# Four graph networks in one kernel: one of DVE's two inputs moved from SBUF to PSUM in layer 0 and the attentions

## The reference, cut to what matters

```
L0: msg = relu(x[src] + edge_attr @ We + be);  h = x + segment_sum(msg, dst);  gelu(h@W1+b1)@W2+b2
L1: four attentions (8 heads; 16, 32, 16, 64 channels) with batch norms between:
      e = leaky_relu(s_src[src] + s_dst[dst]);  m = segment_max(e, dst);  ex = exp(e - m[dst])
      alpha = ex / segment_sum(ex, dst)[dst];   out = segment_sum(h[src] * alpha, dst)
L2: five steps of m = (h @ W[type])[src];  a = segment_sum(m, dst);  h = gru(a, h)
L3: relu(segment_sum((h @ W16[type])[src] * weight, dst))
```

## Time and profile before

| stage | from, to (us) | us | POOL busy | PE busy | DVE busy | granted PE clock |
|---|---|---|---|---|---|---|
| layer 0 | 75 to 1170 | 1095 | 848 | 684 | 640 | 0.57 |
| attention a, pass | 1325 to 2423 | 1098 | 851 | 497 | 388 | 0.73 |
| attention b, pass | 2677 to 3823 | 1146 | 900 | 638 | 481 | 0.79 |
| attention c, pass | 4099 to 5184 | 1085 | 838 | 497 | 371 | 0.73 |
| attention d, pass | 5439 to 7282 | 1843 | 1463 | 1125 | 709 | 0.77 |
| layer 2 (steps) | 7640 to 9350 | 1710 | 0 | 1650 | 355 | 0.95 |
| layer 3, pass | 9445 to 10452 | 1007 | 761 | 314 | 333 | 0.62 |

### The profile page before, as it was taken

One profiled execution on the slowest core, in us unless ns is written; L12 is line 12 of the kernel. 1 busy time (PEld: TensorE's weight loads), 2 busy tenths in 40 slices (PEclk: granted clock), 3 DMA queues, 4 the chain that ended last, 5 costly groups with the idle time before them and its releaser, 6 DMA issues. The chain is left out here.

```text
span 10484.5 us, 120372 instructions
## 1 busy us (share of the span) xinstructions
PE 6178.0 (59%) x43869; PEld 5573.6 (53%) x43869; DVE 4046.9 (39%) x8325; ACT 2190.6 (21%) x5754; POOL 6356.2 (61%) x5804
## 2 busy tenths in 40 slices
PE   4666534444455545444446666665699999993333
PEld 3555434443455534444436665665488888862322
DVE  6656433335344453333453334333422211223333
ACT  0000022221233320322213333333011100111111
POOL 5777677776777775777767777776400000007776
PEclk7555567775787875777757777777599999975666
DMA  5555522220333321222124444443087788751111
GB/s 176 173 188 173 80 53 59 58 59 17 94 102 101 102 61 30 58 59 58 47 62 121 121 120 120 120 120 97 4 321 289 280 315 308 288 195 28 27 27 27
DMA packets 451604, 1241.90 MB, mean 118 GB/s; under 512 B 157362, under 2 KB 233139, under 8 KB 411041
## 3 DMA queue, kind: packets, MB, share of 16 engines
q1 hardware_dynamic: 213988, 744.49, 20.2%
q0 software_dynamic: 237024, 489.72, 17.9%
HBM read 1096.42 MB, written 137.35 MB: 118 GB/s over the span
## 5 line engine op out<-in xcount | busy, mean ns | idle before, releaser
L1122 PE MATMUL ps<-pool 128*106 128x128 f32 (+2 forms) x19344 | 2707.5, 311 | 266.5 <-DVE pool L1029 266.5
L1122 PEld LDWEIGHTS ps<-pool 128*106 128x106 f32 (+2 forms) x19344 | 2678.1, 193 | 279.0 <-DVE pool L1029 278.6
L441 POOL DMA_INDIRECT pool<-t,ACC x416 | 392.6, 944 | 1963.0 <-issue 1963.0
L1080 ACT ACTIVATE ACC<-ps 72x256 f32 (+1 forms) x2418 | 1010.3, 418 | 2271.2 <-PE ps L1122 2058.5
L718 POOL DMA_INDIRECT cnt_d<-pool x806 | 1064.8, 1321 | 540.2 <-PE ps L1299 221.5
L1102 PE MATMUL ps<-ident,pool 128*128 128x128 f32 (+1 forms) x204 | 96.3, 472 | 2080.7 <-DVE pool L989 2080.7
L1102 PEld LDWEIGHTS ps<-ident,pool 128*128 128x128 f32 (+1 forms) x204 | 37.0, 181 | 2129.6 <-DVE pool L989 2129.6
L1147 POOL DMA_INDIRECT pool<-d_h,srcT_s x806 | 943.1, 1170 | 245.5 <-issue 231.2
L1147 POOL DMA_INDIRECT pool<-b_h,srcT_s x806 | 899.4, 1116 | 245.5 <-issue 234.9
L1147 POOL DMA_INDIRECT pool<-a_h,srcT_s x806 | 850.9, 1056 | 245.6 <-issue 245.0
L1147 POOL DMA_INDIRECT pool<-c_h,srcT_s x806 | 836.8, 1038 | 245.6 <-issue 245.3
(11 more groups left out here) (258 smaller groups left out, 7910.5 us busy)
## 6 DMA issues: line engine op xcount, KB each, us to landing
ACC<-cnt_d SPq DMA_DIRECT2D x206, 1600.0 KB, 8.5
pool<-cnt_d SPq DMA_DIRECT2D x104, 1600.0 KB, 8.6
cnt_d<-pool SPq DMA_DIRECT2D x31, 3200.0 KB, 14.6
pool<-key_d SPq DMA_DIRECT2D x62, 832.0 KB, 6.3
pool<-seg_d SPq DMA_DIRECT2D x204, 64.5 KB
cnt_d<-pool POOLq DMA_INDIRECT x806, 2.5
pool<-a_h,srcT_s POOLq DMA_INDIRECT x806
pool<-b_h,srcT_s POOLq DMA_INDIRECT x806
```

What stands on the lines that cost most here:

```text
L441: g.indirect_dma_start(out=gb[b][:, k, :], out_offset=None, in_=table, in_offset=bass.IndirectOffsetOnAxis(ap=idx[:, c:c + 1], axis=0)).th ...
L1080: a.activation(win[:, 0:NPL, bass.ds(reg, 128)], pl[0].rearrange("p (i c) -> p i c", c=128), ACT.Copy).then_inc(*(tile_out if last else A) ...
L1122: mm = t.matmul(o, gbr[:, tile % RT, M * i:M * i + M], oh, start=True, stop=True)
```

## The change

In layer 0 the one-hots read `count0`, a copy of `iota` in bank 5 of PSUM, and the multiplicities read `unit0`, ones in that bank. Bank 5 is then no longer free for products: `tensor_products` and `vector_add_windows` take a number of banks, five in layer 0 and six in layer 3 as before. In the attentions the one-hots read a copy of `iota` in bank 7, and the weights times the multiplicities go to `wp` in bank 7; the multiplies of the rows (L1029) read them there, and one more copy brings them to the rows. PE's turned scores (`eR`, `dR`) and turned weights and maxima (`pC`, `mC`) now share bank 6, and the turn of `sdl` waits for `packed` as well. Each attention and layer 0 copy `iota` once at their start.

```diff
+        count0, unit0 = ps[5][:, 0:128], ps[5][:, 128:256]
         def vector_multiplicity(gi):
-                                       scalar=keyT[:, c:c + 1], in1=onec[:, 0:1].to_broadcast([128, 128]),
-                                       op0=ALU.is_equal, op1=ALU.mult, accum_out=cmul[:, c:c + 1]).then_inc(*V.one())
+                                       scalar=keyT[:, c:c + 1], in1=unit0, op0=ALU.is_equal, op1=ALU.mult, accum_out=cmul[:, c:c + 1]).then_inc(*V.one())
-        def vector_add_windows(gi, FA, o, added):
+        def vector_add_windows(gi, FA, o, added, banks):
-                bk = (NC_ * gi + c) % 6
+                bk = (NC_ * gi + c) % banks
         def tensor_products(gi, msg, oh, FA, o, added, banks):
-                if u >= 6:
-                    t.wait_ge(added.sem, u - 5)
+                if u >= banks:
+                    t.wait_ge(added.sem, u - banks + 1)
-                    mm = t.matmul(ps[u % 6][0:FA, ...
+                    mm = t.matmul(ps[u % banks][0:FA, ...
         def vector_l0():
+            v.tensor_copy(count0, iota[:, :]).then_inc(*V.one())
+            v.memset(unit0, 1.0).then_inc(*V.one())
+            v.wait_ge(*V.now())
-                vector_onehot(gi, oh0, o_l0, iota[:, :])
+                vector_onehot(gi, oh0, o_l0, count0)
             def vector_table():
+                v.tensor_copy(count, iota[:, :]).then_inc(*V.one())
+            eR, dR = ps[6][:, 0:128], ps[6][:, 128:256]
+            pC, mC = ps[6][:, 256:384], ps[6][:, 384:512]
+            count, wp = ps[7][:, 0:128], ps[7][:, 128:256]
             def vector_edge_onehot(c, n):
-                v.tensor_tensor(out=ohr[:, k:k + n, :], in0=iota[:, :].unsqueeze(1).to_broadcast([128, n, 128]),
+                v.tensor_tensor(out=ohr[:, k:k + n, :], in0=count.unsqueeze(1).to_broadcast([128, n, 128]),
             def vector_edge_weights(gi):
-                v.tensor_tensor(out=rows[:, :, 0:8], in0=ps[6][:, 0:8 * n].rearrange("p (k h) -> p k h", h=8),
+                wk = wp[:, 0:8 * n].rearrange("p (k h) -> p k h", h=8)
+                v.tensor_tensor(out=wk, in0=pC[:, 0:8 * n].rearrange("p (k h) -> p k h", h=8),
                 v.wait_ge(*V.now())
+                v.tensor_copy(rows[:, :, 0:8], wk).then_inc(*V.one())
-                                        in1=rows[:, q:q + n_, 0:8].unsqueeze(3).to_broadcast([128, n_, 8, C]),
+                                        in1=wk[:, q:q + n_, :].unsqueeze(3).to_broadcast([128, n_, 8, C]),
             def tensor_turn_scores(gi):
                 t.wait_ge(lists_g[b].sem, l0[b] + 32 * (gi // 2 + 1))
-                t.transpose(ps[7][0:8 * n, 128:256], sdl[:, b, 0:8 * n], ident[:, :])
                 t.wait_ge(packed.sem, pk0 + gi + 1)
-                t.transpose(ps[7][0:8 * n, 0:128], sc[:, b, 0:8 * n], ident[:, :]).then_inc(*eT.one())
+                t.transpose(dR[0:8 * n, :], sdl[:, b, 0:8 * n], ident[:, :])
+                t.transpose(eR[0:8 * n, :], sc[:, b, 0:8 * n], ident[:, :]).then_inc(*eT.one())
```

More of the change, by code:

```diff
@@ L451, in vector_onehot, with tensor_products @@
                             op=ALU.is_equal).then_inc(*o["oh"].one())
-        def tensor_products(gi, msg, oh, FA, o, added):
+        def tensor_products(gi, msg, oh, FA, o, added, banks):
             b = gi % 2
@@ L456, in tensor_products @@
                 u = NC_ * gi + c
-                if u >= 6:
-                    t.wait_ge(added.sem, u - 5)
+                if u >= banks:
+                    t.wait_ge(added.sem, u - banks + 1)
                 for i in range(m):
-                    mm = t.matmul(ps[u % 6][0:FA, 128 * i:128 * i + 128], msg[:, k0 + i, :], oh[b][:, k0 + i, :],
+                    mm = t.matmul(ps[u % banks][0:FA, 128 * i:128 * i + 128], msg[:, k0 + i, :], oh[b][:, k0 + i, :],
                                   start=True, stop=True)
@@ L998, in vector_edge_logits @@
                 v.wait_ge(eT.sem, et0 + gi + 1)
-                v.tensor_tensor_scan(out=e, data0=sg[:, 0:128], data1=ps[7][0:r, 128:256], initial=iniT[0:r, gi:gi + 1],
+                v.tensor_tensor_scan(out=e, data0=sg[:, 0:128], data1=dR[0:r, :], initial=iniT[0:r, gi:gi + 1],
                                      op0=ALU.add, op1=ALU.max).then_inc(*V.one())
                 v.wait_ge(*V.now())
-                v.tensor_tensor(out=e, in0=e, in1=ps[7][0:r, 0:128], op=ALU.add).then_inc(*V.one())
+                v.tensor_tensor(out=e, in0=e, in1=eR[0:r, :], op=ALU.add).then_inc(*V.one())
                 v.wait_ge(*V.now())
@@ L1108, in tensor_turn_back @@
                 t.wait_ge(logit.sem, lg0 + gi + 1)
-                t.transpose(ps[6][:, 128:128 + r], ml[0:r, :], ident[0:r, 0:r])
+                t.transpose(mC[:, 0:r], ml[0:r, :], ident[0:r, 0:r])
                 t.wait_ge(prob.sem, pb0 + gi + 1)
-                t.transpose(ps[6][:, 0:r], et[0:r, b, :], ident[0:r, 0:r]).then_inc(*mxT.one())
+                t.transpose(pC[:, 0:r], et[0:r, b, :], ident[0:r, 0:r]).then_inc(*mxT.one())
             def tensor_tile(tile):
@@ L1567, in vector_step_pass @@
                 if gi:
-                    vector_add_windows(gi - 1, D, o, added)
-            vector_add_windows(NG - 1, D, o, added)
+                    vector_add_windows(gi - 1, D, o, added, 6)
+            vector_add_windows(NG - 1, D, o, added, 6)
             v.wait_ge(*added.now())
@@ L1586, in tensor_step_pass @@
                 t.wait_ge(o["msg"].sem, gi + 1)
-                tensor_products(gi, gb[gi % GB], oh, D, o, added)
+                tensor_products(gi, gb[gi % GB], oh, D, o, added, 6)
             t.wait_ge(*added.now())
```

8 lines of the change are left out of this document (4 added, 4 removed).

## The result

The changed kernel takes 9876.11 us (median of four runs, 9873.66 to 9878.19) against 10490.87 us for the kernel before beside it. The ratio is 0.9413, with a 95% interval of 0.9397 to 0.943. The profiled execution has a span of 9874.2 us against 10484.5: 610.3 us less.

What follows compares the result with a forecast made beforehand. POOL sets the pace, its gathers held by DVE instructions reading SBUF twice. Attentions 495 + layer 0 10 - 2 = 503 us off 10485.76 gives 9983, and 9985 as the runs' median; range 9890 to 10070 us.

Steps and rivals of the forecast that it cites:

- What bounds the kernel: Layer 0 and the four attention passes: POOL's gathers and scatters, busy plus 0.30 us each, set the pace of all five.
- That one input in PSUM ends the holds: Attention one-hots and L1029 stop holding POOL's gathers: 63, 125, 64 and 243 us in a to d, 495 in all.
- rivals 4 and 5: 4: L1029 still holds POOL, 10280 us, chance 0.05; 5: POOL held by DVE's writes or its long run, 10540, 0.02.
- What PSUM costs DVE: Layer 0's multiplicities with a PSUM input: no extra time taken; bounds 10% of 351 ns each, 23 us in the stage.
- rival 2: Layer 0: a PSUM input costs each multiplicity 70 ns, 0.9 us a group, 46 us less gain: 10031 us; chance 0.06.
- The slack of the chain: Attention passes: the chain from scores to tiles grows 0.5 us a group but stays hidden, 3.7 us left in d.
- rival 3: Attention d becomes bound by its chain, 50 to 100 us less gain: 10035 to 10085 us; chance 0.07.
- I take 10: Layer 0's gain of 10 us: with five banks PE's loop of 17.8 us, not POOL's 16.2, sets the pace.
- rival 1: POOL sets layer 0's pace too, as PE's clock rises or the loop closes earlier: gain 577, 9911 us; chance 0.12.
- lower bound of the scans: Attention passes: holds left by scans and similar short instructions at 0 us a group, +48 us on the gain.
- 12 us a pass: Attentions: holds left by L1004, L1006, L1009 and L1012, still reading SBUF twice, 0.24 us a group x 51.
- what lies between the stages: A loss of 2 us in all: the chain's added 0.5 us shows behind the last group of each pass.

Runs made afterwards that it cites:

- experiment 5: Changed kernel with the attentions' one-hots, or else only the multiplies' weights, read from SBUF again; 11473.29 and 11338.94 us beside the changed kernel's 11272.19, in the long condition.
- experiment 2: Kernel before with five banks in place of six for layer 0's products, nothing else changed; 10488.62 us beside 10482.69.
- Experiment 4: Changed kernel with two idle 128 x 128 copies on DVE ahead of the first scan of every group in the attentions; 9875.03 us.
- long condition: Chips or times at which every kernel took 7 to 8% longer; kernel before 11230 to 11370 us in place of 10490; the change's ratio there 0.9918.

## Why the prediction was wrong in size and right in kind

**What bounds the kernel: right.** POOL's busy time fell, its idle time moved by under 1 us in each of the five stages, and the end followed.

**That one input in PSUM ends the holds: right,** rivals 4 and 5 fall. The gathers that took 1.68 to 2.42 us are 0.94 to 0.97, and experiment 5 brings either hold back alone. In layer 0 the one-hots and the multiplicities were changed together; the gathers that began during a multiplicity took 1.03 us in the mean before (176 of them) and 0.945 after (163). The rule of the Trainium skill that two SBUF inputs contend with a GpSimd instruction that reads SBUF ("SBUF — State Buffer", "Who interferes with whom") agrees; its inferred sentence that `tensor_tensor` doesn't stall DMAs does not (279 us of holds by L1029's form).

**What PSUM costs DVE: right at nothing,** rival 2 falls. L313 takes 342 ns with `unit0` in PSUM, where L311 took 351; L1042 1212 against 1220; L450 1878. The 65 ns more that the prediction estimated from the Trainium skill ("VectorE: DVE Perf Modes", section on the TRN2 errata) are in none of these lines.

**The slack of the chain: right,** rival 3 falls. DVE still waits for the gather ahead of the scores in each of 50 groups a pass, though less (us, times), to be set beside 380.8 in the earlier trace rows:

```profile
  DMA pool<-d_h,srcT_s: 527.6, 50
...
  DMA pool<-b_h,srcT_s: 221.7, 50
```

In b 7.6 us a group became 4.4, for a period shorter by 134 / 50 = 2.7 and the half microsecond of the chain.

**First step that failed: layer 0, "I take 10".** The structure was right: one bank less makes the last chunk wait for the third chunk's adds, L609 or L614 releases 51 groups, and at the lower level the turn takes 17.8 us. Mis-sized was the duration of L609 in it. I took 5.81 us from a turn in which PE had idled 1.70 us ahead of its last two chunks, and named as a bound, with a chance of 0.12, that it might run at 2.4 GHz without that gap. It did so for the most part in 33 of the first 51 groups: 3.1 to 3.8 us, 3.60 in the turn shown (not the 2.9 of the prediction's half, and so a loop of mostly 15.0 to 15.8 us and not 14.9). POOL's 16.2 then set the pace: 86 us, the bound being 84. This is rival 1, and it is 76 of the 107 us by which the spans' difference (610) was missed.

The prediction held the stage's mean granted clock, 0.57, against rival 1. It rose only to 0.59, so it spoke against nothing. The clock had been at 2.4 GHz for 130 us before, but only 20 of them fell on L609; what changed is where they fall (experiment 2). "The clock rises in PE's longer run", as rival 1 has it, is therefore right in its outcome and not shown as a mechanism.

**The range's lower end** was also added up wrongly. "Rival 1 with the lower bound of the scans" is 9911 - 48 = 9863 by the prediction's own terms, and not 9890; the measured 9876 lies between the two.

**Second step: "12 us a pass" for the scans.** The passes gained 10.6, 9.5, 11.6 and 9 us more than forecast, 41 together of the 48 that four times 12 make; some 4 us of holds by short instructions are left. In the timeline of before the scans did hold a gather in each group of b (0.18 us), and nothing was changed in them. What changed is when they meet. In b before, the gather that met L1006 began 0.05 us behind it, group after group: a gather held until a one-hot of DVE has ended starts its successors at a fixed distance from DVE's next instructions. Without these holds the distance varies: in b after, 49 gathers began 0.04 to 0.18 us behind L1015. One of them:

```profile
3013.18 0.29 DVE L1015 SCALAR_TENSOR_TENSOR pool<-pool 128x128 f32<-128x128 f32 x1
3013.29 0.99 POOL L1160 DMA_INDIRECT pool<-b_h,srcT_s  x1 [0.30 <-issue]
3013.50 0.42 DVE L1017 TENSOR_TENSOR_SCAN pool<-pool 128x128 f32<-128x128 f32 x1
```

It began 0.11 us behind L1015 and was held by 0.05 us, and L1017, which began 0.21 us behind the gather, did not hold it. The kernel of experiment 5 with the one-hots' holds back shows the scan's hold again: 32 gathers beside L1017 in b at 1.12 us in the mean, as before. With the multiplies' holds alone it is 0.99. Experiment 4 moved the scans, and with them which pass is held, so that the size depends on the meeting is shown. That the one-hots' hold sets the meeting is what those two means suggest and is not shown: in a of experiment 4, 48 gathers were held by a scan with no one-hot holding anything.

**Third: what lies between the stages,** 11 us lost and not 2. Seven of them stand ahead of pass a, in the first gathers of the scores, before (first line) and after:

```profile
L943 POOL DMA_INDIRECT small<-a_d,dst x7 | 6.7, 952 | 8.3 <-DMA a_d<-sdn 6.5 <-issue 1.8
```

```profile
L949 POOL DMA_INDIRECT small<-a_d,dst x7 | 6.7, 951 | 15.7 <-DMA a_d<-sdn 13.9 <-issue 1.8
```

The transfer of `sdn` used to be nearly through when layer 0's last gathers ended; POOL now comes earlier and waits for it 13.9 us in place of 6.5. The other 4 us are spread over three transitions and were not looked into.

The terms close: 74 + 134 + 76 + 252 + 86 - 11 = 611, against 610.3 us of span.

## What to carry to other kernels

Where POOL issues gathers back to back, look for gathers longer than their median and for the DVE instruction beside them: if that reads two inputs from SBUF, one of them in PSUM frees POOL, at no cost to DVE here. Before the price of a longer chain on PE is taken from the timeline, look at the granted clock of the row and of the idle time ahead of it, and not at the stage's mean: a row at the lower level behind a gap at the higher one doesn't price the same work without the gap. Where a forecast keeps something back for short instructions that hold a gather, look at when the two meet: that decides how much they hold, and a change to the long holds can move it.

## What the runs showed that was not expected

- Giving PE less room made a part of its work faster: with one bank less, a matmul of the edges' products takes 349 ns in the mean where it took 402, with nothing else changed, and 328 with the change; with the gap put back 385. In the kernel before, half of the time at 2.4 GHz in layer 0 (65 of 130 us) had passed while PE was idle.
- Whether a gather is held depends on when it starts. In layer 0 before, those that began 0.13 us or more ahead of the one-hot took 0.94 to 0.95 us, those that began with it or up to 0.29 us behind took 2.4 to 2.7, and of six in between, 0.07 to 0.12 us ahead, four took 2.8. A held gather ends about 0.8 us after DVE's instruction does: 0.82 us beside the one-hot of the earlier trace rows, 0.76 beside the scan of the earlier trace rows, 0.81 behind L1015 above.
- In the long condition the same change is worth 94 us in place of 615, and half of it costs 99. Time per instruction of DVE and POOL is nearly unchanged there; waits ahead of the instructions are longer.
